# Attention loops: 3 to 7 of a step's 27 differences of exponentials on GpSimd, its other work reordered

## What is computed

```python
xn, ln = layernorm(context), layernorm(latents)      # context (16, 1601, 128), latents (16, 64, 128)
q = ln @ Wq
k, v = split(concat([xn, ln], axis=1) @ Wkv)
logits = einsum('bhld,bhsd->bhls', q * s, k * s)     # second layer: masked context rows get -max
w = softmax(logits)
out = einsum('bhls,bhsd->bhld', w, v) @ Wo
```

## Time and profile before

| | |
|---|---|
| median of 3 runs | 2065.31 us (2063.27 to 2069.19) |
| profiled execution | 2067.51 us, its span 2065.6 us |
| busy: TensorE, VectorE, ScalarE, GpSimd | 1914.6, 1682.6, 1250.5, 898.2 us |
| unmasked loop, 16 steps | from 74 to 837 us of the span |
| masked loop, 16 steps | from 1146 to 1897 us of the span |
| VectorE's differences, L1260 | 864, 583.9 us, 682 ns each |

### The profile page before, as it was taken

How to read it: one execution, slowest core, us unless ns; L and a number is a source line. 1 busy time by engine, 2 the same in 40 slices (tenths; PEclk the granted TensorE clock), 3 DMA queues, 4 the chain that set the end, 5 groups by cost and what they waited for, 6 DMA issues and landing times. The chain is left out here.

```text
span 2065.6 us, 34989 instructions
## 1 busy us (share of the span) xinstructions
PE 1914.6 (93%) x12326; PEld 1037.9 (50%) x12326; DVE 1682.6 (81%) x3999; ACT 1250.5 (61%) x2237; POOL 898.2 (43%) x951
## 2 busy tenths in 40 slices
PE   7899999999999999899788999999999999998786
PEld 6444544444454544433656545454545454544585
DVE  6889889889989896699666788879797978786657
ACT  4466666665757666444244676867777777776312
POOL 5576565666666652088231424333232323232004
PEclk9899999999999999989998999999999999999898
DMA  4332222222222220132104011211121111110100
GB/s 140 89 105 65 70 67 68 67 68 68 73 73 68 51 67 1 48 115 89 40 1 126 14 38 39 50 39 38 39 59 36 41 39 39 38 30 1 29 1 10
DMA packets 148854, 110.53 MB, mean 54 GB/s; under 512 B 120892, under 2 KB 136232, under 8 KB 148680
## 3 DMA queue, kind: packets, MB, share of 16 engines
q1 hardware_dynamic: 148680, 108.31, 18.8%
HBM read 65.15 MB, written 14.29 MB: 38 GB/s over the span
## 5 line engine op out<-in xcount | busy, mean ns | idle before, releaser
L1260 DVE TENSOR_TENSOR x_p_lo<-x_psum,x_p_hi 128x512 f16<-128x512 f32 (+1 forms) x864 | 583.9, 682 | 110.6 <-ACT x_psum L1022 109.8
L1021 ACT ACTIVATE x_p_hi<-x_psum 128x512 f16<-128x512 f32 (+1 forms) x448 | 268.2, 599 | 260.3 <-PE x_psum L865 210.3
L1021 ACT ACTIVATE x_p_hi<-x_psum,x_bcol 128x512 f16<-128x512 f32 (+1 forms) x416 | 289.7, 696 | 153.9 <-PE x_psum L865 151.9
L891 PE MATMUL x_psum<-x_p_hi,x_x_both 128*128 128x512 f16 (+1 forms) x832 | 317.1, 381 | 30.4 <-DVE x_p_lo L1260 29.5
L863 PE MATMUL x_psum<-x_q,x_xT_both 128*128 128x512 f16 x832 | 316.3, 380 | 3.0 <-DMA x_q<-x_shift_rows 3.0
L892 PE MATMUL x_psum<-x_p_lo,x_x_both 128*128 128x512 f16 (+1 forms) x832 | 315.7, 379 | 0.0
L893 PE MATMUL x_psum<-x_p_hi,x_x_both 128*128 128x512 f16 (+1 forms) x832 | 315.6, 379 | 0.0
L865 PE MATMUL x_psum<-x_q,x_xT_both 128*128 128x512 f16 x832 | 315.6, 379 | 0.0
L864 PE MATMUL x_psum<-x_q,x_xT_both 128*128 128x512 f16 x832 | 315.6, 379 | 0.0
L1199 DVE CUSTOM_DVE_ANT_0 x_junk<-x_psum,x_brow 128x512 bf16<-128x512 f32 (+2 forms) x512 | 279.3, 584 | 8.8 <-PE x_psum L942 6.7
L1202 DVE TENSOR_REDUCE x_mx<-x_psum 128x1 f32<-128x512 f32 (+2 forms) x512 | 276.6, 583 | 2.2 <-PE x_psum L942 1.1
(11 more groups left out here) (486 smaller groups left out, 3609.8 us busy)
## 6 DMA issues: line engine op xcount, KB each, us to landing
x_x_both<-context_rows SPq DMA_DIRECT2D x32, 832.0 KB, 5.3
context_rows<-x_x SPq DMA_DIRECT2D x16, 832.0 KB, 3.5
x_raw<-in_ctx SPq DMA_DIRECT2D x16, 768.0 KB
ssm_c_row<-ssm_bc_rows SPq DMA_DIRECT2D x16, 512.0 KB, 4.2
ssm_b_wide<-ssm_bc_rows SPq DMA_DIRECT2D x7, 512.0 KB, 3.5
x_mrow<-in_mask_BxS_bk SPq DMA_DIRECT2D x16, 200.1 KB
x_Wkv<-in_L_xattn_Wkv SPq DMA_DIRECT2D x4, 512.0 KB, 5.3
x_xT_both<-context_rows SPq DMA_TRANSPOSE x96, 4.0
```

The costliest lines, as they stand in the source:

```text
L891: pe.matmul(out, v_hi, p_hi[r][rows, :], start=start, stop=False)
L1021: act.activation(p_hi[r][rows, :], score[r][rows, :], ACT.Exp, scale=SCORE_UNIT, **bias).then_inc(p_hi_ready, 1)
L1260: v.tensor_tensor(p_lo[r][rows, :], score[r][rows, :], p_hi[r][rows, :], ALU.subtract).then_inc(p_lo_ready, 1)
```

## The change

Of each step's 27 differences some go from VectorE to GpSimd: in the unmasked loop units 10, 13 and 16 of even and 8, 11, 14, 17 and 20 of odd steps, in the masked loop 9, 11, 13, 15, 17 and 8, 10, ... 20. For these ScalarE writes the fp32 exponential into one of two SBUF buffers `p32` and not over the scores; it waits until GpSimd has read that buffer before. TensorE's scores then wait for the exponential of the unit that had the bank, its products for GpSimd's difference (`p_lo_pool`). VectorE leaves these units out.

GpSimd's order changes in the unmasked loop. In even steps `sums_parted` (in step 0 `weights_parted`) stands ahead of `context_normal`, and the three differences ahead of the tiles 0, 4 and 8. In odd steps the differences stand ahead of the tiles 4 and 8, behind the tiles, between two pieces of the rest in `halves` (blocks 0 to 6 and 7 to 12), and behind it, and `sums_parted` comes last. In the masked loop, and in the last pair of the unmasked one, the differences stand behind `sums_parted`.

```diff
-        def halves(pool, n):
+        def halves(pool, n, between=None):
...
+            if between is None:
+                pool.tensor_tensor(x16[:, 1, :, :], xt[:, :, :], x16[:, 0, :, :], ALU.subtract).then_inc(x16_ready, 1)
+                return
+            pool.tensor_tensor(x16[:, 1, 0:FRONT, :], xt[:, 0:FRONT, :], x16[:, 0, 0:FRONT, :], ALU.subtract)
+            between()
+            pool.tensor_tensor(x16[:, 1, FRONT:KT, :], xt[:, FRONT:KT, :], x16[:, 0, FRONT:KT, :], ALU.subtract).then_inc(x16_ready, 1)
...
             for j in range(KT):
+                among(j)
                 ins = normal_tile(pool, j, par)
...
+    p32 = [sb(f"p32_{k}", [P, HALF]) for k in range(2)]
...
+    BY_POOL = (((10, 13, 16), (8, 11, 14, 17, 20)), ((9, 11, 13, 15, 17), (8, 10, 12, 14, 16, 18, 20)))[masked]
...
-                    pe.wait_ge(p_lo_ready, half + user_before(u) + 1)
+                    v = user_before(u)
+                    if by_pool(par if v >= 0 else 1 - par, v % STEPS):
+                        pe.wait_ge(p32_ready, half + v + 1)
+                    else:
+                        pe.wait_ge(*lows_made(b, v))
...
-                pe.wait_ge(p_lo_ready, at.half + u + 1)
+                pe.wait_ge(*lows_made(at.b, u))
...
-                act.activation(score[r][rows, :], score[r][rows, :], ACT.Exp, scale=SCORE_UNIT, **bias).then_inc(p32_ready, 1)
+                whole = score[r]
+                if by_pool(at.par, u):
+                    made = lows_made(at.b, u)[1] - 1
+                    whole = p32[made % 2]
+                    if made > 1:
+                        act.wait_ge(p_lo_pool, made - 1)
+                act.activation(whole[rows, :], score[r][rows, :], ACT.Exp, scale=SCORE_UNIT, **bias).then_inc(p32_ready, 1)
...
+            def probability_lows(at, units):
+                for u in units:
+                    made = lows_made(at.b, u)[1] - 1
+                    wait_alone(pool, p32_ready, at.half + u + 1)
+                    low(p32[made % 2][:, :], p_lo[u % RING][:, :], p_hi[u % RING][:, :]).then_inc(p_lo_pool, 1)
...
-                if at.has_next2 and not masked:
-                    context_normal(pool, wait_alone, at.b + 2, at.par)
-                    halves(pool, at.b + 2)
+                def some_lows():
+                    probability_lows(at, lows[:1])
+                    del lows[:1]
+
                 if at.first and at.par == 0:
                     weights_parted()
-                else:
+                elif masked or at.par == 0 or not at.has_next2:
+                    sums_parted(at)
+                if at.has_next2 and not masked:
+                    def among(j):
+                        if j in ((0, 4, 8), (4, 8))[at.par]:
+                            some_lows()
+
+                    context_normal(pool, wait_alone, at.b + 2, at.par, among)
+                    if at.par:
+                        some_lows()
+                    halves(pool, at.b + 2, some_lows if at.par else None)
+                probability_lows(at, lows)
+                if at.has_next2 and not masked and at.par:
                     sums_parted(at)
...
-                    v.wait_ge(p32_ready, at.half + u + 1)
-                    v.tensor_tensor(p_lo[r][rows, :], score[r][rows, :], p_hi[r][rows, :], ALU.subtract).then_inc(p_lo_ready, 1)
+                    if not by_pool(at.par, u):
+                        v.wait_ge(p32_ready, at.half + u + 1)
+                        v.tensor_tensor(p_lo[r][rows, :], score[r][rows, :], p_hi[r][rows, :], ALU.subtract).then_inc(p_lo_ready, 1)
```

More of the change, by code:

```diff
@@ L232, in halves @@
             wait_alone(pool, x_hi_ready, n + 1)
-            pool.tensor_tensor(x16[:, 1, :, :], xt[:, :, :], x16[:, 0, :, :], ALU.subtract).then_inc(x16_ready, 1)
+            if between is None:
[4 more added lines that the diff above has]
+            pool.tensor_tensor(x16[:, 1, FRONT:KT, :], xt[:, FRONT:KT, :], x16[:, 0, FRONT:KT, :], ALU.subtract).then_inc(x16_ready, 1)
         x_step = [None]
@@ L294, in normal_tile, with context_normal @@
                                      ALU.subtract, ALU.mult)
-        def context_normal(pool, wait, n, par):
+        def context_normal(pool, wait, n, par, among=lambda j: None):
             if not (isinstance(n, int) and n == 0):
@@ L593, in attention_loop, with by_pool, lows_made @@
     part_high, sum_parted, vo_parted = sem("part_high"), sem("sum_parted"), sem("vo_parted")
+    p_lo_pool = sem("p_lo_pool")
+    BY_POOL = (((10, 13, 16), (8, 11, 14, 17, 20)), ((9, 11, 13, 15, 17), (8, 10, 12, 14, 16, 18, 20)))[masked]
+    POOL_EACH = sum(len(x) for x in BY_POOL)
+    def by_pool(par, u):
+        return u in BY_POOL[par]
+    def lows_made(b, u):
+        if u < 0:
+            b, u = b - 1, u + STEPS
+        pool = (b // 2) * POOL_EACH + (len(BY_POOL[0]) if b % 2 else 0) + sum(k <= u for k in BY_POOL[b % 2])
+        return (p_lo_pool, pool) if by_pool(b % 2, u) else (p_lo_ready, b * STEPS + u + 1 - pool)
     def user_before(u):
@@ L1141, in body @@
             def body(at):
+                lows = list(BY_POOL[at.par])
                 if at.has_next:
```

## The result

The changed kernel takes 2121.36 us (median of 4 executions, 2116.47 to 2133.01), the one before 2067.25 in the same comparison: a ratio of 1.0262 with a 95% interval from 1.0216 to 1.0307. The forecast was 2089 with a range to 2105. The profiled execution of after is its slowest, 2133.01 us with a span of 2131.1, 65.5 us longer than the 2065.6 of before. By the medians the difference is 54.1 us (2.6%), so some 11 us of the table belong to this one execution, and no trace shows in which steps they lie.

A forecast was written before the change was run, and what follows sets the result against it. TensorE was taken to set the pace in mid-step, with VectorE nearly full but waiting. Against 2067.5 us: +24.0 statistics, +2.1 unit 13, -2.0 step 0, +0.4 last steps, -0.8 masked, giving 2091.2, as a median 2089; range 2061 to 2105.

The forecast's parts named there:

- the largest term: Unmasked even steps 2 to 12: GpSimd's sums hold VectorE's statistics, 4.0 us a step, 24 us, bounds 14 and 30.
- the walk of the dearer case: Unmasked even steps, cast first: L257, L260, L262 each wait for one GpSimd operation; TensorE stands 3.0; in all 5.0 us.
- SyncE's cover: End of unmasked even steps: shift rows leave at 308, the next step begins at 315, covered by some 3 us.
- the freed time is waited away: Unmasked steps: VectorE spends the time freed by moved differences waiting for the max matmul; cost at nothing.
- The cheaper walk: Unmasked even steps, L257 ahead of the first cast: L259 and L262 wait, TensorE stands for 1.95; 2.3 us.
- unit 13's difference: Even steps: GpSimd's difference delays L1207; 2.1 us in seven unmasked steps, 2.8 taken back in eight masked ones.
- the lateness of the forecast: Unmasked even steps: GpSimd's halves, for which store_x in SyncE's queue waits, end some 8.4 us later.
- The masked gain: Masked loop: differences moved off VectorE gain 0.45 us per pair, 3.6 in eight; bounds nothing and 1.8 each.
- the sum of rows 3: Kernel before: TensorE's waits at L891 for late differences, 29.5 us in 50 places, the longest 3.1.
- the rivals: Whole kernel: statistics hardly held 0.16 (2059 to 2068), odd steps stall too 0.13 (2096 to 2112), faster 0.11, VectorE not relieved.
- Faster: Rival, chance 0.11: VectorE carries freed time into the turn and units 22 to 24, halving 29.5 us of waits; 2050.

The follow-up runs named there:

- the order alone: Changed kernel with every difference left on VectorE, so only GpSimd's new order remains: 2100.19 us, ratio 1.0162 to the kernel before.
- without the overlap: Changed kernel, but in unmasked even steps from 2 on GpSimd starts the sums only after VectorE's statistics: 2092.49 us, ratio 1.0124 to the kernel before.
- the weights kernel: Changed kernel, but in the first masked step the split of the value weights stands behind GpSimd's five differences: median 2119.7 us.
- Without unit 13: Changed kernel, but unit 13's difference of even steps stays on VectorE, in both loops: 2137.84 us, ratio 1.0342 to the kernel before.
- the offload alone: Changed kernel, but unmasked even steps' sums and step 0's weights go back behind the context; the 160 differences stay on GpSimd: 2137.86 us, ratio 1.0337.
- the first guess moved: Changed kernel, but in unmasked even steps from 2 on VectorE makes L271, L78 and L80 two units later: 2107.84 us, ratio 1.0201.

## Why the prediction was wrong, point by point

The direction was right, and so was the mechanism of the largest term. The size was not: the range ended at 2105, and the median lies 16 us above it. Three steps of the prediction failed in the main: the walk of the dearer case ended too early, SyncE's cover was not there, and the first masked step was put at about nothing.

**Right.** That the freed time is waited away: five of the seven masked odd steps are the same to 0.02 us with seven differences fewer on VectorE. That the statistics are held: in five of the six even steps in the order of the dearer walk (L262, L265 and L267 of after, one GpSimd operation each), with a stand of 2.4 to 2.9 us at unit 3 in all six for the forecast's 3.0. The cheaper walk came true in the order alone, with a stand of 1.99 for 1.95 and 3.2 to 4.5 us a step for its 2.3 and up to 1.7 of halved clock. That its six steps add up to the very 24 of the term is luck of one execution, in which every step fell on the cheap side. That unit 13's difference holds the operation on constant rows: 0.28 at unit 12 in unmasked, 0.35 in masked even steps for 0.3 and 0.35. That GpSimd's busy time would rise by 185 us (188). VectorE's fell by 47 and not by 109: its held operations count as busy, some 5 us more in each even step from L261 to L271.

**The size of the even step: 8.7 us instead of 4.0.** Two pieces of the sum failed here.
- The dear walk, put at 5.0, ended at the late difference. "The rest of the statistics and four maxima" were put at 0.35 us in the cheap walk and at 0.3 in this one. But the first of that rest, L271, is held too (1.75 us, and 0.17 without the overlap), and the maximum behind it frees the bank for which the max matmul waits: a second stand of 2.0, and the halved clock for 2.5 us and not up to 1.7. So a dear step cost 6.3 to 7.6 us up to unit 6, in after and in the weights kernel. Taking L271 out of the overlap gave 3.75 us a step back between the two traces, some 2.5 by the medians. The Trainium skill ("SBUF — State Buffer", section "Who interferes with whom") says that a tensor_scalar can enter a two-port mode and contends then; the prediction gave its sum as 30 us in a sentence by itself. Here the trace agrees with the page (L271's 1.75), and the 30 were still too few, since only a hold was added and not what waits for the bank.
- SyncE's cover, "some 3 us", did not exist. The shift rows were set against the start of the next step, 315.0. But TensorE makes scores three units ahead. In the kernel before, the first scores that need them start 2.1 us ahead of that:

```profile
312.91 0.38 PE L863 MATMUL x_psum<-x_q,x_xT_both 128*128 128x512 f16 x1
```

SyncE and then TensorE at the end of step 2 of after:

```profile
220.05 0.36 SPq L215 DMA_DIRECT2D context_rows<-x_x  x1
...
226.56 0.36 SPq L198 DMA_DIRECT2D x_x_both<-context_rows  x1
226.99 0.68 SPq L805 DMA_DIRECT2D x_q<-x_shift_rows  x1
```

```profile
233.14 0.39 PE L889 MATMUL x_psum<-x_q,x_xT_both 128*128 128x512 f16 x1 [1.41 <-DMA x_q<-x_shift_rows]
```

The halves are ready 40.3 us into step 4 and 24.3 before: 16.0, of which 7.7 are TensorE's own loss ahead of them and 8.3 the lateness of the forecast (8.4). The 6.9 us from L215 to the shift rows' issue are its 6.6. But they are needed 2.1 us earlier than it said, and they were under way for 6.15 us (226.99 to 233.14) where its 3 us of cover left them four, a figure that no row of it shows. In a masked odd step of the kernel before they took 2.0 (issued at 1424.92, first scores at 1426.94). Here the next step's context, 832 KB, was issued 0.43 us ahead of them and landed at 232.90, 0.24 us before TensorE went on; in the four even steps with a wait 4.8 to 6.6 us passed so. That this load holds them up was not tested. The waits cost 7.0 us in four steps. In step 0 the weights' new place gives 4.0 (43.60 with the order alone), and the changed kernel waits 3.6 for the shift rows and 0.7 at unit 21 and runs the start and the end of the step at the halved clock: 49.62. L1274 took 1.12 there and not 3.62.

**The first masked step: 6.3 us that were not in the sum.** The prediction moved the weights' split only in the unmasked loop, where it moves. In the masked one its place is the same and the differences come behind it: unit 9's waits for 12 us of weights. In front of an engine that works in order, what stands there already is part of an added operation's price.

**The masked gain, 3.6 us, was nothing.** It was estimated from the sum of rows 3. Read unit by unit, TensorE's waits in a masked step of the kernel before lie at unit 24 (0.47 in even and 0.41 in odd steps) and, in odd ones, at unit 6 (0.66) and at the turn (0.41); of the offloaded units none is among them. Without unit 13 an even step gained 0.14.

**Odd steps, -2.9 us, by chance.** GpSimd's output additions (before L759) held L259 in these. Where an even step stood for its shift rows, the additions were over earlier and the odd step behind it is 0.8 to 1.3 shorter. The loss gave a part of itself back. Step 5 alone grew, by 1.15: SyncE's queue was late there as well, and TensorE waited 1.07 for the shift rows.

**The preamble, +6.3 us, is not explained by the change.** VectorE's L520 and GpSimd's L234, in code that is the same in both kernels; first before, then after:

```profile
29.64 1.24 DVE L514 TENSOR_TENSOR x_lnT_lo<-x_lnT,x_lnT_hi 128x1024 f16<-128x1024 f32 x1
```

```profile
29.78 4.33 DVE L520 TENSOR_TENSOR x_lnT_lo<-x_lnT,x_lnT_hi 128x1024 f16<-128x1024 f32 x1
```

GpSimd's operation starts at 29.88 before and at 29.68 after. Where VectorE was first it took 1.2 to 1.65 us (ten of twelve kernels, first step at 74.8 to 78.4 us); where GpSimd was first VectorE waited for its end (the changed kernel, 81.4, and the one with the offload alone, 80.2). What moved the start by 0.2 us was not found. The hold itself is 3.1 of the 6.3 us; the way of the rest was not traced.

Of the rivals none came true. "Faster" named the right waits but not the way to them: the differences have to be moved at the units where TensorE waits.

## What to carry to other kernels

Ask of each operation that is to be moved whether the pacing engine waits for it, unit by unit: 160 differences moved at units without a wait gained 0.14 us a step at most, 16 moved at the one with a wait gained 0.65 us in each of 14 steps. Where a moved block stalls another engine, follow that engine's program past the first late result, until everything behind it is on time again, and set a transfer against its first reader, which may belong to the next step's work done ahead. On an engine that works in order, an added operation pays for everything that stands ahead of it, and so does all that stands behind.

## What the runs showed of the hardware

- Two operations that start 0.01 to 0.02 us apart on VectorE and GpSimd can go either way: behind the same subtraction L265 took 0.17 us in some steps and 2.13 in others of one kernel, and with that a step lost some 4 or some 7 us. A place where such a pair meets has two prices, and one trace shows one of them.
- The holding is mutual. Ahead of the first step GpSimd's subtraction (L233, after it L234) took 4.20 us where it started behind VectorE's L514 or L520, and 3.35 where it was first.
- The granted clock behind a stand of 2.0 to 2.9 us fell to the 1.2 GHz level in some steps and not in others of one kernel (three and three with the first guess moved; four and two in the order alone, each behind 2.0); with a second stand of 1.3 to 1.7 us behind it, it fell in all six steps of the changed kernel.
